# Cross attention in a decoder layer: the softmax row sums of seven of eight batches take a way through memory and are inverted on 128 rows of 32

## What is computed

```python
q = _split_heads(x @ qw + qb)          # 8 batches, 256 queries, 16 heads of 8
k = _split_heads(ctx @ kw + kb)        # 1601 context rows
v = _split_heads(ctx @ vw + vb)
scores = jnp.einsum('bqhd,bkhd->bhqk', q, k) / np.sqrt(D // H) + mask
probs = jax.nn.softmax(scores, axis=-1)
out = jnp.einsum('bhqk,bkhd->bqhd', probs, v)
```

## Time and profile before

| what | value |
|---|---|
| median of 3 runs | 1305.81 us (1302.74 to 1306.11) |
| span of the profiled execution | 1324.9 us |
| its own time outside the span | not recorded; the span is all that the profile gives |
| busy in the span: PE, DVE, ACT, POOL | 1104.3, 1018.2, 869.6, 403.8 us |
| mean busy share of the 16 DMA engines, queue of SP | 25.1% |
| L1449, reciprocal of 128x256, 8 times | 14.1 us, 1757 ns each |
| L228, matmuls of `head_sums` in cross attention | 382 ns each, overlapping |

### The profile page before, as it was taken

The page is one execution under the profiler, slowest core; times in us unless marked ns, Lnnn a source line. Parts: engine busy times, 40 slices in busy tenths (PEclk is TensorE's granted clock), DMA queues, the critical chain, the costliest instruction groups (busy, mean ns, idle before and its releaser), DMA issues. The chain is left out here.

```text
span 1324.9 us, 33276 instructions
## 1 busy us (share of the span) xinstructions
PE 1104.3 (83%) x12028; PEld 602.7 (45%) x12028; DVE 1018.2 (77%) x2779; ACT 869.6 (66%) x1764; POOL 403.8 (30%) x832
## 2 busy tenths in 40 slices
PE   5799995699999999999999999986688878178894
PEld 2344443244444444444444444433344436167773
DVE  7488857588889898898988889956699968755554
ACT  3488873187887878788788787882488744233443
POOL 3211113223050320405023040021624227545552
PEclk9699997699999999999999999997799989588997
DMA  6970005513232132311323113002740022111113
GB/s 164 213 144 30 2 2 138 133 56 84 67 82 68 39 93 84 72 57 34 101 78 81 49 30 85 21 2 58 149 87 2 2 96 72 56 29 39 39 37 111
DMA packets 76648, 92.31 MB, mean 70 GB/s; under 512 B 8463, under 2 KB 62711, under 8 KB 76488
## 3 DMA queue, kind: packets, MB, share of 16 engines
q1 hardware_dynamic: 72392, 83.90, 25.1%
q0 software_dynamic: 2496, 5.12, 1.5%
q10 hardware_dynamic: 1600, 1.18, 0.3%
HBM read 64.37 MB, written 27.02 MB: 69 GB/s over the span
## 5 line engine op out<-in xcount | busy, mean ns | idle before, releaser
L1436 DVE TENSOR_REDUCE MG<-bank 128x1 f32<-128x401 f32 (+1 forms) x1024 | 515.4, 566 | 75.3 <-PE bank L1220 73.6
L1356 ACT ACTIVATE PT<-bank 128x512 f32<-128x512 f32 (+1 forms) x624 | 334.6, 597 | 64.3 <-PE bank L1238 63.8
L1238 PE MATMUL bank<-QP,KP 54*128 54x256 bf16 (+1 forms) x1664 | 252.4, 274 | 16.3 <-DVE CAT L1451 4.1
L1220 PE MATMUL bank<-KP,QP 54*128 54x401 bf16 (+1 forms) x1024 | 237.0, 344 | 14.8 <-DMA KP<-ctx_k_parts 9.6
L1258 PE MATMUL bank<-PT,VP 128*9 128x256 f32 (+1 forms) x2688 | 197.3, 367 | 0.8 <-ACT XT L1356 0.8
L1511 POOL TENSOR_TENSOR MP<-MN,ZERO 128x4 bf16<-128x4 f32 x128 | 26.4, 206 | 440.8 <-DVE MN L1443 435.8
L1238 PEld LDWEIGHTS bank<-QP,KP 54*128 54x128 bf16 (+1 forms) x1664 | 110.4, 96 | 108.3 <-ACT PT L1356 24.4
L1220 PEld LDWEIGHTS bank<-KP,QP 54*128 54x128 bf16 x1024 | 75.5, 94 | 125.0 <-DVE MG L1436 94.4
L1356 ACT ACTIVATE XT<-bank 128x512 f32<-128x512 f32 (+1 forms) x208 | 116.2, 599 | 20.3 <-PE bank L1238 19.9
L896 PE MATMUL bank<-QP,KP 51*128 51x256 bf16 x512 | 95.7, 281 | 33.6 <-ACT QP L827 8.8
L1258 PEld LDWEIGHTS bank<-PT,VP 128*9 128x9 f32 (+1 forms) x2688 | 76.0, 90 | 57.6 <-issue 20.4
(11 more groups left out here) (281 smaller groups left out, 2007.5 us busy)
## 6 DMA issues: line engine op xcount, KB each, us to landing
KP<-ctx_k_parts SPq DMA_DIRECT2D x128, 100.1 KB
ctx_k_parts<-KPARTS SPq DMA_DIRECT2D x16, 600.4 KB
KP<-ctx_k_parts SPq DMA_DIRECT2D x128, 59.4 KB
CN<-in_ctx SPq DMA_DIRECT2D x8, 768.0 KB
RAW<-in_w_gate_up SPq DMA_DIRECT2D x8, 512.0 KB, 3.8
QP<-q_parts SPq DMA_DIRECT2D x20, 192.0 KB
ctx_k_parts<-KPARTS SPq DMA_DIRECT2D x16, 200.1 KB
UQ<-bias_table SPq DMA_DIRECT2D x4, 768.0 KB, 8.5
```

The source lines that it names most:

```text
L1220: nc.tensor.matmul(GRAIN[n % NG][:, 0:w], k.QP[half, p, b * S + 128 * qt:b * S + 128 * (qt + 1)], k.KP[half, p, a:a + w], start=True, stop ...
L1238: return nc.tensor.matmul(bank[0:rows[t], S * at:S * (at + 1)], k.KP[half, p, 128 * t:128 * t + rows[t]], k.QP[half, p, b * S:(b + 1) * S] ...
L1356: nc.scalar.activation(PT[n % NP][0:rows[t], :], bank_of("s", g, t)[0:rows[t], :], ACT.Exp).then_inc(exp_done, 1)
L1436: nc.vector.tensor_reduce(MG[:, g % 4, 2 * s + qt, chunk:chunk + 1], GRAIN[n % NG][:, 0:w], AX.X, ALU.max).then_inc(m_read, 1)
```

## The change

The values keep their way over TensorE, but alone (8 matmuls, moved from step 0 to step 2 of the next batch). The four rows of sums of each pair are sent from `OT` to memory (`take_sums`, 4 rows of 256 each, 8 times a batch); the two halves are read back as 128 rows of 32 (`spread_sums`), added and inverted on VectorE in step 1 (`reciprocals`), sent to memory (`give_reciprocals`) and read back spread over each head's eight rows (`place_reciprocals`); VectorE multiplies in step 2 (`scale`). SyncE issues all of these transfers. The last batch keeps the old way (`last_values`, `divide_last`).

```diff
         if j in (5, 10) and rounds:
             plan.append(rounds[j // 10])
-        if j == 1 and p == 0:
-            plan.append(("c", 0, 0))
+        if j == 1 and p < 3:
+            plan.append((("e", "r", "c")[p], 0, 0))
...
-            elif what == "c":
-                if b > 0:
+            elif what in "rc":
+                if 0 < b < B:
+                    actions[what](b - 1, i)
+            elif what == "e":
+                if b == B:
                     actions[what](b - 1, i)
...
-            def batch_sums(b, i):
+            def batch_values(b, i):
                 pe.wait_ge(o_read, PAIRS * (b + 1))
-                head_sums(k, take_bank("c", b, i), lambda g: OT[:, g % NO, :], b).then_inc(sums_turned, 1)
+                head_sums(k, take_bank("c", b, i), lambda g: OT[:, g % NO, :], b, (0,)).then_inc(sums_turned, 1)
...
                     act.wait_ge(sums_turned, (g - NO) // PAIRS + 1)
+                    act.wait_ge(sums_out, 16 * PAIRS * ((g - NO) // PAIRS + 1))
                 nc.scalar.copy(OT[:, g % NO, :], k.PO[:, 0:S]).then_inc(o_read, 1)
...
-            def divide(b, i):
-                bank = bank_of("c", b, i)
+            def reciprocals(b, i):
+                v.wait_ge(sums_in, 32 * (b + 1))
+                nc.vector.tensor_tensor(SUMS[:, 2, :], SUMS[:, 0, :], SUMS[:, 1, :], ALU.add).then_inc(sums_added, 1)
+                v.wait_ge(sums_added, b + 1)
+                if b > 0:
+                    v.wait_ge(rec_out, 16 * b)
+                nc.vector.reciprocal(SUMS[:, 3, :], SUMS[:, 2, :]).then_inc(compact_done, 1)
+
+            def scale(b, i):
+                v.wait_ge(rec_in, 16 * (b + 1))
                 v.wait_ge(sums_turned, b + 1)
+                nc.vector.tensor_tensor(k.CAT[:, b * S:(b + 1) * S], bank_of("c", b, i)[:, 0:S], REC[:, :],
+                                        ALU.mult).then_inc(sums_done, 1)
...
+            def take_sums(g):
+                b, p = batch_of(g)
+                sp.wait_ge(o_read, g + 1)
+                if p == 0 and b > 0:
+                    sp.wait_ge(sums_in, 32 * b)
+                sp.dma_start(k.dHalves.ap()[p], OT[HD:128:32, g % NO, :]).then_inc(sums_out, 16)
+
+            def spread_sums(b):
+                sp.wait_ge(sums_out, 16 * PAIRS * (b + 1))
+                if b > 0:
+                    sp.wait_ge(compact_done, b)
+                for half in range(2):
+                    src = bass.AP(tensor=k.dHalves.ap().tensor, offset=2 * S * half,
+                                  ap=[[4 * S, PAIRS], [SEGMENT, 2 * S // SEGMENT], [1, SEGMENT]])
+                    sp.dma_start(SUMS[:, half, :], src).then_inc(sums_in, 16)
+
+            def give_reciprocals(b):
+                sp.wait_ge(compact_done, b + 1)
+                if b > 0:
+                    sp.wait_ge(rec_in, 16 * b)
+                sp.dma_start(compact(k.dRec), SUMS[:, 3, :]).then_inc(rec_out, 16)
+
+            def place_reciprocals(b):
+                sp.wait_ge(rec_out, 16 * (b + 1))
+                if b > 0:
+                    sp.wait_ge(sums_done, b)
+                src = bass.AP(tensor=k.dRec.ap().tensor, offset=0, ap=[[S, H], [0, HD], [1, S]])
+                sp.dma_start(REC[:, :], src).then_inc(rec_in, 16)
+
+            def finish_sums(b):
+                take_sums(PAIRS * (b + 1) - 1)
+                spread_sums(b)
+                give_reciprocals(b)
+                place_reciprocals(b)
...
             for b in range(LAST_BATCH):
+                if b > 0:
+                    finish_sums(b - 1)
                 sp.wait_ge(ctx_turned, 4 * (b + 2))
...
                     load_keys(b + 1, p)
+                    if p > 0:
+                        take_sums(PAIRS * b + p - 1)
...
+            finish_sums(LAST_BATCH - 1)
```

More of the change, by code:

```diff
@@ L150, in allocate @@
     k.dYS = dram("expert_rows", [2 * TOK + 128 * SLOT_TILES, D], F32)
+    k.dSums = dram("head_sums", [H, S], F32)
+    k.dRec = dram("head_reciprocals", [H, S], F32)
+    k.dHalves = dram("half_sums", [PAIRS, 4, S], F32)
     k.dMask = dram("mask_parts", [3, B * NCTX], BF16)
@@ L220, in batch_of, with head_sums @@
     return divmod(g, PAIRS)
-def head_sums(k, bank, slot_of, b):
-    for kind in range(2):
+def head_sums(k, bank, slot_of, b, kinds=(0, 1)):
+    for kind in kinds:
         for parity in range(2):
@@ L231, in head_sums, with compact @@
     return last
+SEGMENT = H * S // 128
+def compact(dram):
+    return bass.AP(tensor=dram.ap().tensor, offset=0, ap=[[SEGMENT, 128], [1, SEGMENT]])
 def join_and_measure(k, v, g, out, projected, other, sems):
@@ L1117, in cross_ring @@
     turns = [(what, 0, i) for what in "TKV" for i in range(4)]
-    cross_steps({what: lambda unit, i, what=what: turns.append((what, unit, i)) for what in "smcTKV"})
+    cross_steps({what: lambda unit, i, what=what: turns.append((what, unit, i)) for what in "smceTKV"})
     return turns
@@ L1155, in phase_cross @@
         REC = k.sb("REC", [128, S], stack=st)
+        SUMS = k.sb("SUMS", [128, 4, SEGMENT], stack=st)
         ZERO = k.sb("ZERO", [128, 1], stack=st)
@@ L1169, in phase_cross @@
         o_read, sums_turned, rec_done, sums_done = sem("o_read"), sem("sums_turned"), sem("rec_done"), sem("sums_done")
+        sums_out, sums_in, sums_added = sem("sums_out"), sem("sums_in"), sem("sums_added")
+        compact_done, rec_out, rec_in = sem("compact_done"), sem("rec_out"), sem("rec_in")
         qk_in = [sem(f"qk_in{c}") for c in range(4)]
@@ L1195, in take_bank @@
                         pe.wait_ge(m_rows, a + 1)
-                    elif old == "c":
+                    elif old in "ce":
                         pe.wait_ge(sums_done, a + 1)
@@ L1271, in max_rows, with last_values @@
                 last.then_inc(m_turned, 1)
-            def batch_sums(b, i):
+            def batch_values(b, i):
                 pe.wait_ge(o_read, PAIRS * (b + 1))
-                head_sums(k, take_bank("c", b, i), lambda g: OT[:, g % NO, :], b).then_inc(sums_turned, 1)
+                head_sums(k, take_bank("c", b, i), lambda g: OT[:, g % NO, :], b, (0,)).then_inc(sums_turned, 1)
+            def last_values(b, i):
+                pe.wait_ge(o_read, PAIRS * (b + 1))
+                head_sums(k, take_bank("e", b, i), lambda g: OT[:, g % NO, :], b).then_inc(sums_turned, 1)
             def turn_context(b, i):
@@ L1343, in _ @@
                 make_values(0, i)
-            cross_steps({"s": scores, "h": last_tile, "g": grain, "v": values, "m": max_rows, "c": batch_sums,
-                         "T": turn_context, "K": make_keys, "V": make_values})
+            cross_steps({"s": scores, "h": last_tile, "g": grain, "v": values, "m": max_rows, "c": batch_values,
+                         "e": last_values, "T": turn_context, "K": make_keys, "V": make_values})
         @block.scalar
@@ L1444, in negate, with divide_last @@
                                         negate=True).then_inc(neg_ready, 1)
-            def divide(b, i):
-                bank = bank_of("c", b, i)
-                v.wait_ge(sums_turned, b + 1)
+            def reciprocals(b, i):
[7 more added lines that the diff above has]
+                v.wait_ge(rec_in, 16 * (b + 1))
+                v.wait_ge(sums_turned, b + 1)
+                nc.vector.tensor_tensor(k.CAT[:, b * S:(b + 1) * S], bank_of("c", b, i)[:, 0:S], REC[:, :],
+                                        ALU.mult).then_inc(sums_done, 1)
+            def divide_last(b, i):
+                bank = bank_of("e", b, i)
+                v.wait_ge(sums_turned, b + 1)
+                v.wait_ge(sums_done, b)
                 nc.vector.reciprocal(REC[:, :], bank[:, S:2 * S]).then_inc(rec_done, 1)
-                v.wait_ge(rec_done, b + 1)
+                v.wait_ge(rec_done, 1)
                 nc.vector.tensor_tensor(k.CAT[:, b * S:(b + 1) * S], bank[:, 0:S], REC[:, :],
@@ L1502, in _ @@
                 take_values(0, i)
-            cross_steps({"g": maxima, "neg": negate, "c": divide, "V": take_values})
+            cross_steps({"g": maxima, "neg": negate, "r": reciprocals, "c": scale, "e": divide_last, "V": take_values})
         @block.gpsimd
```

## The result

The changed kernel takes 1413.51 us (median of 4 runs, 1410.92 to 1416.2) against 1304.3 us: a ratio of 1.0843 with a 95% interval of 1.0821 to 1.0865. It is 109 us slower; the forecast added 138, with a range that holds the measured time.

What follows compares the result with a forecast made beforehand. TensorE and VectorE, both nearly full in cross attention, were taken as the bound, so stalls hit the whole pipeline. 1305.8 + 121 (waits) + 21 (clock) + 3.5 (VectorE) - 8 (division) = 1443 us, range 1388 to 1478.

Steps and rivals of the forecast that it cites:

- The first rival: Sums overtake the tail on idle engines, only SyncE's program order counts: 52 us of stall, 1362 us; chance 0.13.
- The second rival: Clock stays low 25 us instead of 8 after stalls, 70 us in place of 21: 1492 us; chance 0.09.
- The third: Rival: sums are back before VectorE asks, the shorter division shows alone: 1301 us; chance 0.04.
- the waits: VectorE's wait for sums in step 1 stalls the pipeline: four of 15 and three of 20.4, 121 us.
- the clock: Low clock when work resumes after each stall: 3 us per stall, 21 us, bounds 0 and 38.
- add and reciprocal of 128x32: Added work on nearly full VectorE: 0.5 us per batch, 3.5 us in all, bounds 2 and 5.
- the shorter division: Reciprocal of 128x256 and 8 of 16 matmuls go, in seven batches: gain 8 us, bounds 3 and 12.
- What the change removes: Prediction's part on the division: costs 2.17 us in step 0, what moves to step 2 costs 1.0; gain 8 us.
- the sums ahead and the acknowledgement: Behind the tail: 1 us for seven sums further ahead in line, 1 us until the last one's data is acknowledged.

Runs made afterwards that it cites:

- the late question: Changed kernel with add and reciprocal in step 3 instead of 1, values and multiplication in step 4 instead of 2, 12 OT slots: 1290.27 us, 0.9893.
- without trips: Changed kernel without any transfer of sums and reciprocals, dividing by ones in seven batches: 1288.29 us, 0.9868 of the kernel before.
- the clock held: Changed kernel with 14 to 22 extra unread matmuls on TensorE filling each of the seven stalls nearly whole: 1405.81 us, 1.0775 of the kernel before.

## Why the prediction was right, and where its sizes were off

The mechanism came as forecast: VectorE waits at the `SUMS` add, seven times, longer in batches 1, 3 and 5, because the sums stand in one line with 19-row loads that one of sixteen engines works off. The runs with split loads show it by taking the line away, the late question by waiting it out, the moved query loads by shortening it. The rule of the Trainium skill on the number of engines ("DMA: Bandwidth & Descriptors", "Why a DMA increments its semaphore by 16 and not by 1") agrees: 19 rows, which no number from 2 to 16 divides, make the tail, at a DMA share of 0.06 to 0.07; 16 and 3 rows do not.

The first rival (only SyncE's own order counts) fails in even batches: 11.1 us go by between issue and landing with SyncE idle. In odd ones it has half a point, since 11.2 of 20 us pass before SyncE is done issuing; but that is in part the same line, since with the split loads SyncE is done at 340.09 and the wait is 0.3. The second rival (a clock that stays low for 25 us) did not come: the clock is back 4.6 to 7.0 us after work resumes in six stalls, and after 14.7 in batch 4, where step 2 took 13.16 us. The third needs the line gone, and then comes true with more than its 5 us.

By the terms of the sum:

| term | forecast | measured |
|---|---|---|
| the waits | 121 us | 113.0 |
| the clock | 21 | at most 14.8: the steps take 127.8 more than without trips, less 113.0; all but 2.9 goes with the clock held |
| add and reciprocal of 128x32 | 3.5 | 0 in step 1 |
| the shorter division | -8 | -16 with the line above; the steps show 14.9, of which 1.3 is the dip of the earlier trace rows |
| sum | 138 | 112; the runs say 109 |

All four terms were off to the same side, so nothing cancelled in the sum. The one that the prediction misread from its rows is "What the change removes": step 1 was taken as the twin of step 0 without a division, 9.63 us. Without it step 0 takes 9.26, so the division cost 2.54 us and not 2.17. And what moved to step 2 costs 10.37 - 9.77 = 0.60 there, not 1.0; that makes 7 x (2.54 - 0.60) = 13.6 us, not 8. In the same way the 3.5 us for VectorE were counted on a full engine, and the step shows that it had that time to spare.

Of the waits, the way up to the landing of the sums was put too long. In batch 2 it was 16.5 us by forecast from the last key load's issue (445 - 430.50 for the tail, and 1 + 1 for the sums ahead and the acknowledgement, for which the prediction had no row); it took 14.6 (447.21 to 461.83), and no row parts this into tail and sums. From the landing to the add it was 3.1 by forecast and 2.6 measured (461.83 to 464.43). Together that is 2.4 us less, of which 0.4 is given back by VectorE coming sooner. In batch 1 the forecast of 20.4 met 20.0 partly by luck: VectorE came 11.2 us before SyncE was done issuing, where 8.5 were forecast, and the sums landed 6.0 us behind that, where 8.8 were forecast.

The prediction's 7 to 8 us of low clock behind each stall came from no row. In six stalls it lasted 4.6 to 7.0, and the sum of 51 us comes near only through the 14.7 of batch 4. Its price was lower too: in batch 2, 1.6 us for 5.6 us at 0.50, 0.29 per us, and over all seven 14.8 for 51, 0.29 again, where one dip in the trace of before had given 0.39.

The kernel that beats both is the change with split loads, 1281.88 us. Of its 22 us, 6.5 come with the split alone and the rest with the shorter division.

## What to carry to other kernels

Before results are sent on a round trip through a transfer queue, look at what stands in that queue at that moment and how long after its last issue it still runs; a mean DMA share of 0.24 did not show that one engine would still be busy 14 us after the last issue. The loads of 19 rows were worth splitting even in the kernel where nobody waited at the ends of batches (6.5 us), and worth far more (132 us) once other transfers stood behind them in the same queue. And when a piece of work is taken out of a step, its price is found by a run of that step without it, not by a neighbour that looks alike.

## What the runs showed of the hardware beyond that

Issuing into a queue with transfers in line held the issuing engine (no row shows how many such a queue takes): four rows of sums (4 KB) took SyncE up to 3.74 us to issue behind the key and query loads and 0.53 us with the tail gone. A second queue was not shielded from the first: 7.6 us from the end of the issue to the use of 32 KB beside the tail, at most 3.8 without it, and 1.4 on SyncE's own queue with the loads split. And low clock was cheaper in this mixed pipeline than its ratio says: at half clock the steps lost 0.29 to 0.39 us per us, not 0.5.
